# The first batch's W2 products in a four-stage residual kernel: rounded part first, remainder part later

## The reference, cut to what matters

```
x = x + quantise(x)                       # 8 groups: clip(round(x/d)+zp)..., chosen by |x| <= threshold
x = x + x @ W1[a(b)].T                    # W1: 8 matrices of 1024x1024, one chosen per batch
x = x + x @ W2.T + (x @ lora_A[l(b)]) @ lora_B.T * 0.5
x = x + (x @ B3[a(b)].T) @ A3[a(b)].T
```

## Time and profile before

| what | value |
|---|---|
| runs of the kernel before | median 486.1 us (485.64 to 488.54, 3 runs) |
| the profiled execution's own time | 486.4 us |
| its span | 484.6 us, 8214 instructions |
| busy: PE, DVE, ACT | 465.8 us (96%), 418.6 us (86%), 359.5 us (74%) |
| moved by the transfers | 67.07 MB |

### The profile page before, as it was taken

One profiled execution on the slowest core, in us unless ns is written; L12 is line 12 of the kernel. 1 busy time (PEld: TensorE's weight loads), 2 busy tenths in 40 slices (PEclk: granted clock), 3 DMA queues, 4 the chain that ended last, 5 costly groups with the idle time before them and its releaser, 6 DMA issues.

```text
span 484.6 us, 8214 instructions
## 1 busy us (share of the span) xinstructions
PE 465.8 (96%) x3184; PEld 426.1 (88%) x3184; DVE 418.6 (86%) x480; ACT 359.5 (74%) x384; POOL 45.2 (9%) x46
## 2 busy tenths in 40 slices
PE   3999769999999999999999999999999999999997
PEld 3969669899898989899998989899999989899995
DVE  3999999988999899989999899989999899989120
ACT  5989968679787879679787879679787879676011
POOL 1054001200003000200002000200002000100000
PEclk9999979999999999999999999999999999999999
DMA  7997314712236113712326113712336123702002
GB/s 276 402 415 243 131 34 148 292 45 103 90 95 284 43 60 131 276 60 103 106 91 268 44 62 127 287 49 103 118 93 254 43 73 116 289 5 87 1 1 87
DMA packets 17830, 67.07 MB, mean 138 GB/s; under 512 B 2576, under 2 KB 5904, under 8 KB 13712
## 3 DMA queue, kind: packets, MB, share of 16 engines
q1 hardware_dynamic: 17808, 66.81, 37.7%
HBM read 56.84 MB, written 9.96 MB: 138 GB/s over the span
## 4 chain that ended last, share of the span: by engine, by line
PE 83%; DVE 8%; ACT 4%; DMA 2%; issue 1%; POOL 0%; DVEq 0%; SPq 0%; ACTq 0%
PE x_bank L598 45%; PE acc L623 32%; DVE y L460 4%; PE x_bank L611 3%; PE acc L635 2%; PE acc L633 2%; DVE uq L448 1%; ACT tq L329 1%; DMA ua<-w2t 1%; DMA xin<-x 1%; DVE x L473 1%; DVE uq L466 1%; ACT mask L344 1%; DVE tq L439 1%; ACT w2h L400 1%
## 5 line engine op out<-in xcount | busy, mean ns | idle before, releaser
L598 PEld LDWEIGHTS x_bank<-x,w1b 128*128 128x128 f32 x2048 | 234.4, 194 | 8.1 <-issue 4.4
L598 PE MATMUL x_bank<-x,w1b 128*128 128x128 f32 x2048 | 235.8, 277 | 4.0 <-DVE x L473 4.0
L329 ACT ACTIVATE tq<-xin,magic,rdelta 128x1024 f32<-128x1024 f32 x128 | 157.0, 1234 | 3.7 <-DMA xin<-x 3.4
L344 ACT ACTIVATE mask<-absx,negtop 128x1024 bf16<-128x1024 f32 x112 | 128.5, 1147 | 40.8 <-DVE y L460 40.1
L460 DVE COPY_PREDICATED y<-mask,uq 128x1024 f32<-128x1024 int16 x112 | 150.7, 1346 | 0.1
L439 DVE TENSOR_SCALAR tq<-tq,par 128x1024 f32<-128x1024 f32 x128 | 98.5, 769 | 8.5 <-ACT tq L329 4.8
L448 DVE TENSOR_SCALAR uq<-tq,ylow,yhigh 128x1024 f32<-128x1024 f32 x112 | 92.5, 826 | 1.1 <-issue 0.9
L623 PE MATMUL acc<-w2h,x2h 128*128 128x512 f32 x256 | 80.9, 393 | 3.3 <-DVE x2l L479 3.3
L623 PE MATMUL acc<-w2h,x2l 128*128 128x512 f32 x256 | 79.9, 389 | 0.0
L623 PE MATMUL acc<-w2l,x2h 128*128 128x512 f32 x256 | 79.1, 390 | 0.0
L295 POOL TENSOR_TENSOR w1b<-w1b,eye 128x256 f32<-128x256 f32 x32 | 34.6, 1083 | 370.9 <-DMA w1b<-w 370.9
(11 more groups left out here) (56 smaller groups left out, 219.3 us busy)
## 6 DMA issues: line engine op xcount, KB each, us to landing
w1b<-w SPq DMA_DIRECT2D x32, 1024.0 KB, 6.7
xin<-x SPq DMA_DIRECT2D x16, 512.0 KB, 3.7
out<-outb SPq DMA_DIRECT2D x14, 512.0 KB, 2.8
w1b<-w2n SPq DMA_DIRECT2D x4, 1024.0 KB, 10.8
ring<-w2t SPq DMA_DIRECT2D x6, 512.0 KB, 6.3
ua<-e_dram SPq DMA_DIRECT2D x16, 128.0 KB, 2.5
ua<-w2t SPq DMA_DIRECT2D x2, 512.0 KB, 7.2
va<-la SPq DMA_DIRECT2D x8, 128.0 KB, 2.7
```

The source lines that it names most:

```text
L329: nc.scalar.activation(tq[:, n % TQ, :], flat(xin, c % UN), ACT.Identity, bias=magic[:, 0:1], scale=rdelta[:, g:g + 1]).then_inc(t_ready, 1)
L344: nc.scalar.activation(mask[:, n % MK, :], absx[:, :], ACT.Relu, bias=negtop[:, g:g + 1], scale=1.0).then_inc(mask_ready, 1)
L598: last = nc.tensor.matmul(x2_bank[2 * t + i][:, o % HALF * P:(o % HALF + 1) * P], w1b[:, o, at:at + P], x1[:, t, k, :], start=(o % HALF == ...
```

## The change

1. `stage` is rotated: `ua` is now the last stage. W2's blocks are loaded and rounded in the order 4, 5, 6, 7, 0, 1, 2, 3; then 4, 5, 6, 7 are loaded a second time. A stage is loaded again in the first round when its block is rounded (`w2h_ready`), in the second when the remainder of its block is made.
2. DVE makes no remainder in steps 10 to 13. It makes them in the order 3, 0, 1, 2, 4, 5, 6, 7 at steps 18, 19, 20, 21, 22, 26, 26, 27.
3. `ACT_V, DVE_V` go from 14, 15 to 17, 18, in every batch.
4. TensorE's first batch does HIGH alone, for both units (unit 0 in the order 0, 1, 2, 4, 5, 6, 7, 3). LOW follows behind unit 1: blocks 3, 0, 1, 2, 4 for both units at the end of the batch, blocks 5, 6, 7 for each unit in batch 1, behind six tiles of its first `w1_x1` and ahead of the `u_low` of that unit. Batch 1 is written out, the loop starts at 2. Batch 1 has six tiles ahead of the `u_low` where the others have three.
5. SP's first batch is written out in a new order; POOL adds four diagonals (the reloaded blocks) between the four of W1 of batch 1.

```diff
-        stage = [ua[:, :]] + [ring[:, i, :] for i in range(ST - 1)]
+        stage = [ring[:, i, :] for i in range(ST - 1)] + [ua[:, :]]
...
+        W2_BLOCK = (4, 5, 6, 7, 0, 1, 2, 3, 4, 5, 6, 7)
+        W2_PLACE = (0, 1, 2, 3, 0, 1, 2, 3, 0, 1, 2, 0)
+        W2_REST = (3, 0, 1, 2, 4, 5, 6, 7)
+        REST_SOON = 5
...
+            def load_w2(i):
+                if ST <= i < KT:
+                    sp.wait_ge(w2h_ready, i - ST + 1)
+                elif i >= KT:
+                    sp.wait_ge(w2l_ready, i - KT + 2)
+                sp.dma_start(stage[W2_PLACE[i]], w2t[W2_BLOCK[i], :, :]).then_inc(stage_in[W2_PLACE[i]], 16)
...
+            sp.wait_ge(x1_ready, 2)
+            load_x(1, 1)
             sp.wait_ge(e_out, 16 * EH)
-            sp.wait_ge(w2l_ready, ST + 1)
+            sp.wait_ge(w2l_ready, 1)
             load_u(a0)
+            a1, lab1 = ids_of(1)
+            for j in range(PAIRS):
+                sp.wait_ge(w1_used, j + 1)
+                load_w1(a1, j)
+                if j < PAIRS - 1:
+                    load_w2(KT + j)
+            sp.wait_ge(vl_ready, 2)
+            load_v(a1, lab1)
+            load_w2(KT + PAIRS - 1)
+            sp.wait_ge(ul_ready, 1)
+            load_u(a1)
+            sp.wait_ge(x1_ready, UN + 1)
+            load_x(2, 0)
...
+            for j in range(PAIRS):
+                w1_diagonal(1, j)
+                if j < PAIRS - 1:
+                    w2_diagonal(KT + j)
+            w2_diagonal(KT + PAIRS - 1)
+            with pool.Fori(2, B) as b:
...
-        ACT_W2, DVE_W2 = (9, 10, 11, 12, 13, 14, 15, 16), (10, 11, 12, 13, 18, 19, 20, 21)
+        ACT_W2, DVE_W2 = 9, (18, 19, 20, 21, 22, 26, 26, 27)
...
-        ACT_V, DVE_V = 14, 15
+        ACT_V, DVE_V = 17, 18
...
+                for at, k in zip(DVE_W2, W2_REST):
+                    if n == at:
+                        i = len(W2_BLOCK) - 1 - W2_BLOCK[::-1].index(k)
+                        dve.wait_ge(w2h_ready, W2_BLOCK.index(k) + 1)
+                        dve.wait_ge(w2_diag, i + 1)
+                        nc.vector.tensor_tensor(w2l[:, k, :], stage[W2_PLACE[i]], w2h[:, k, :].bitcast(f32),
+                                                ALU.subtract).then_inc(w2l_ready, 1)
...
+            def rest(t, order):
+                for i in order:
+                    pe.wait_ge(w2l_ready, i + 1)
+                    product(t, W2_REST[i], LOW)
+
+            def start_batch(b, u_at, second=False):
+                pe.wait_ge(x1_ready, UN * b + 1)
+                w1_x1(b, 0, range(u_at))
+                for t in range(UN):
+                    if second:
+                        rest(t, range(REST_SOON, KT))
+                    u_low(b - 1, 2 * t)
+                    u_low(b - 1, 2 * t + 1)
+                w1_x1(b, 0, range(u_at, OT))
...
+            def first_batch():
+                pe.wait_ge(x1_ready, 1)
+                w1_x1(0, 0, range(OT))
+                pe.wait_ge(g_ready, 2)
+                for k in (0, 1, 2, 4, 5, 6, 7, 3):
+                    if k in (0, HALF):
+                        pe.wait_ge(x2l_ready, k // HALF + 1)
+                    pe.wait_ge(w2h_ready, W2_BLOCK.index(k) + 1)
+                    product(0, k, HIGH)
+                pe.wait_ge(e_ready, 2 * EH)
+                second_unit(0, HIGH, first=True)
+                for k in range(HALF, KT):
+                    product(1, k, HIGH)
+                for t in range(UN):
+                    rest(t, range(REST_SOON))
...
+            first_batch()
+            start_batch(1, 6, second=True)
+            w2_x2(1)
+            second_unit(1)
+            for k in range(HALF, KT):
+                product(1, k)
+            with pe.Fori(2, LAST) as b:
                 batch(b)
-            batch(LAST, last=True)
+            last_batch()
```

More of the change, by code:

```diff
@@ L241, in _, with during @@
                 sp.dma_start(e_dram.rearrange("(h a) r n -> h (a r) n", h=EH)[h], outb[:, h, :]).then_inc(e_out, 16)
+            sp.wait_ge(x1_ready, 2)
+            load_x(1, 1)
             sp.wait_ge(e_out, 16 * EH)
-            sp.wait_ge(w2l_ready, ST + 1)
+            sp.wait_ge(w2l_ready, 1)
             load_u(a0)
-            def during(b, first, second):
+            a1, lab1 = ids_of(1)
[11 more added lines that the diff above has]
+            load_x(2, 0)
+            def during(b, second):
                 a, lab = ids_of(b + 1)
-                if not first:
-                    store(b - 1, 0)
-                    store(b - 1, 1)
+                store(b - 1, 0)
+                store(b - 1, 1)
                 sp.wait_ge(vl_ready, 2 * (b + 1))
@@ L264, in during @@
                     load_x(b + 2, 0)
-            during(0, True, True)
             with sp.Fori(1, LAST - 1) as b:
-                during(b, False, True)
-            during(LAST - 1, False, False)
+                during(b, True)
+            during(LAST - 1, False)
             store(LAST - 1, 0)
@@ L300, in _ @@
                 w2_diagonal(j)
-            for k in range(PAIRS, KT):
-                w2_diagonal(k)
-            with pool.Fori(1, B) as b:
+            for i in range(PAIRS, KT):
+                w2_diagonal(i)
+            for j in range(PAIRS):
[4 more added lines that the diff above has]
+            with pool.Fori(2, B) as b:
                 for j in range(PAIRS):
@@ L396, in tables @@
                                              ACT.Copy).then_inc(g_ready, 1)
[L397 to L400, removed]
+                if ACT_W2 <= n < ACT_W2 + KT:
+                    i = n - ACT_W2
+                    act.wait_ge(w2_diag, i + 1)
+                    nc.scalar.activation(w2h[:, W2_BLOCK[i], :], stage[W2_PLACE[i]], ACT.Copy).then_inc(w2h_ready, 1)
                 for e in range(2 * EH):
@@ L636, in u_low @@
                                  skip_group_check=True).then_inc(acc_done, 1)
-            U_AT = 3
-            def batch(b, first=False, last=False):
-                pe.wait_ge(x1_ready, UN * b + 1)
[L642 to L663, removed]
+            def rest(t, order):
+                for i in order:
+                    pe.wait_ge(w2l_ready, i + 1)
+                    product(t, W2_REST[i], LOW)
@@ new lines, in start_batch, with w2_x2 @@
+            def start_batch(b, u_at, second=False):
+                pe.wait_ge(x1_ready, UN * b + 1)
+                w1_x1(b, 0, range(u_at))
[5 more added lines that the diff above has]
+                w1_x1(b, 0, range(u_at, OT))
+            def w2_x2(b):
+                pe.wait_ge(x2l_ready, BANKS * b + 1)
+                pe.wait_ge(out_ready, ACCS * (b - 1) + 2)
+                for k in range(HALF):
+                    product(0, k)
+                pe.wait_ge(x2l_ready, BANKS * b + 2)
+                for k in range(HALF, KT):
+                    product(0, k)
@@ L664, in batch, with second_unit @@
+            def second_unit(b, parts=ALL, first=False, early=HALF):
                 pe.wait_ge(x1_ready, UN * b + 2)
                 w1_x1(b, 1, range(OT))
[L666 to L669, removed]
                 pe.wait_ge(vl_ready, 2 * (b + 1))
@@ L674, in batch, with last_batch @@
                     pe.wait_ge(out_ready, ACCS * b)
-                early = HALF // 2 if last else HALF
                 for k in range(early):
-                    product(1, k)
+                    product(1, k, parts)
                 pe.wait_ge(x2l_ready, BANKS * b + 4)
                 v_x2(range(HALF, KT))
[L680 to L688, removed]
-                    for k in range(early, KT):
-                        product(1, k)
+            def first_batch():
[13 more added lines that the diff above has]
+                    rest(t, range(REST_SOON))
+            def batch(b):
+                start_batch(b, 3)
+                w2_x2(b)
+                second_unit(b)
+                for k in range(HALF, KT):
+                    product(1, k)
+            def last_batch():
+                early = HALF // 2
+                start_batch(LAST, 3)
+                w2_x2(LAST)
+                second_unit(LAST, early=early)
+                for h in range(2):
+                    for k in range(early, KT):
+                        product(1, k, ALL, (h,))
+                    if h == 0:
+                        u_low(LAST, 0)
+                        u_low(LAST, 1)
+                    u_low(LAST, 2 + h)
             bilinear()
@@ L694, in _ @@
             adapters_e()
-            batch(0, first=True)
-            with pe.Fori(1, LAST) as b:
+            first_batch()
+            start_batch(1, 6, second=True)
+            w2_x2(1)
+            second_unit(1)
+            for k in range(HALF, KT):
+                product(1, k)
+            with pe.Fori(2, LAST) as b:
                 batch(b)
-            batch(LAST, last=True)
+            last_batch()
 def kernel(**inputs):
```

15 lines of the change are left out of this document (3 added, 12 removed).

## The result

The changed kernel takes 495.26 us (median of 4 runs, 494.39 to 495.6), the kernel before 486.07 (median of 4): the ratio is 1.018, 95% interval 1.014 to 1.021. It is slower by 9.2 us, where 489.6 was forecast with a range up to 492.8. The profiled span grew from 484.6 to 493.8 us, by the same 9.2.

The account below looks back on a forecast made before the run. The prediction took TensorE as full from about 73 us on. It summed 0.1 up to batch 1, 2.7 for deferred products and 0.7 for V to +3.5 us, giving 489.6 us, 0.7% slower, range 485.5 to 492.8.

Parts of the forecast that it names:

- What bounds the kernel now: TensorE is full from about 73 us on; only two earlier pauses and a clock loss, 9.7 us at most, can be won.
- Part 1: Ahead of x1 of unit 1: ScalarE's x2h limits, so 1.6 us won and x1 ends at 65.4 instead of 67.0.
- The stage buffer, loaded earlier now: ScalarE ahead of x1 of unit 1: 0.27 us of waiting for the stage buffer would be won.
- Part 2: TensorE until x1 of unit 1: waits about 4.9 us for x1 instead of 3.75, and the 2.7 us clock loss stays.
- Part 3: VectorE up to x1 of unit 2: ends at 99.0, was 97.7; TensorE starts batch 1 0.1 us later.
- Part 4: Batch 1: six deferred products cost TensorE 2.7 us; VectorE's three late remainders fit.
- Part 5: V moved in every batch: 0.13 us a batch, nearly 0.7 for six, ends 0 and 3.2; SP's later loads cost nothing.
- Rival C: V at step 18 costs its full 0.53 us in six batches, 3.2 instead of 0.7: 492.1 us; chance 0.13.
- Part 6: Four reloads adding 2 MB: block 4 is ready between 79 and 81 us, just in time, costed at nothing.
- A: VectorE, not ScalarE, limits ahead of x1 of unit 1; x1 comes 5 us earlier, about 486 us; chance 0.12.
- B: The reload of block 4 comes late, almost 5 us of waiting ahead of x1 of unit 2: 494 us; chance 0.1.
- D: POOL's diagonals hold VectorE out for their whole length, 4.5 instead of 1.2 us before x1 of unit 2: 492.9; chance 0.07.

Follow-up runs that it names:

- e5: e1 with ScalarE's four copies of the E tables moved from steps 12 to 14 to steps 16 and 17; 489.03 us.
- e2: The kernel before with only the V splits of batches 1 to 7 moved to steps 17 and 18; 489.59 us.
- e9: e1 plus four blocks' unit-0 remainder products ahead of the x2l wait, without the six deferred products in batch 1; 490.11 us.
- e3: The changed kernel with SP issuing load_x ahead of the load_v that waits for V, in every loop batch; 492.91 us.
- e1: The changed kernel with the V splits of batches 1 to 7 back at steps 14 and 15; 491.75 us.
- e12: The changed kernel itself, unedited, run again on another occasion; 495.32 us.

## Why the prediction was wrong, point by point

The sum gave 0.1 us up to batch 1, 2.7 in it and 0.7 for V in six batches, 3.5 in all. Measured are 1.9, 2.4 and 4.9, together 9.2. The largest miss is the last term.

- **What bounds the kernel now** held: TensorE is full behind 73 us, and what it is made to wait there is paid.
- **Part 1 (ScalarE limits x1 of unit 1)** was right in mechanism, and e5 showed it. Its size was off: x1 ended at 66.45 instead of 65.4, 0.6 earlier than before. That is the end that the prediction gave for "only the V copies", 66.5. The gain is no larger than the scatter: the changed kernel run again has 67.49, and e2, with the first batch of the kernel before, 65.99. The 0.85 us of ScalarE's waiting that the sum took as won did go, but ScalarE came as much later, as it waited for POOL behind transfers:

```profile
40.58 1.06 ACT L427 ACTIVATE w2h<-ua 128x1024 fp32r<-128x1024 f32 x1 [0.49 <-POOL ua L312]
...
43.15 1.14 ACT L371 ACTIVATE mask<-absx,negtop 128x1024 bf16<-128x1024 f32 x1
...
44.51 1.06 ACT L427 ACTIVATE w2h<-ring 128x1024 fp32r<-128x1024 f32 x1 [0.22 <-POOL ring L312]
...
55.79 0.59 ACT L380 ACTIVATE x2h<-x_bank 128x512 fp32r<-128x512 f32 x1
```

  The mask is back at 43.15 with no wait in front of it, where it was 43.10; ScalarE runs without a break to 55.79 but for 0.22. "The stage buffer, loaded earlier now" failed too: block 0 was issued at 35.14 and added to at 44.02, 8.9 us; before, the block in its place was issued at 37.24 and added to at 42.48. The transfers' share was 0.96 or more from 34 to 42 us, and the earlier issue gave no earlier landing.
- **Part 2** was right about the two pauses in kind (2.16 and 3.16 us, forecast 2.7 and 4.9; the HIGH products between them ran at half clock and so filled the rest) and about the half clock behind them.
- **Part 3** gave 33.56 us from x1 of unit 1 to x1 of unit 2, and 33.58 were measured (33.2 to 34.0 in the other profiles of this program). That it fits so well is partly luck. POOL's eight diagonals stretched VectorE by 1.9 us instead of the former three's 1.05, so by 0.8 and not 1.2 more, and 0.39 us of waiting for block 4's diagonal, put at nothing, made up for it. What it missed is TensorE's own arrival. "That the clock falls or not does not matter here" was said of the first pause; there was a second one, ahead of x2l of unit 1, with a second drop. +1.9 instead of +0.1, of which 1.05 comes from part 1 and 0.8 from this:

```profile
65.23 1.22 DVE L500 TENSOR_TENSOR x<-xin,uq 128x1024 f32<-128x1024 f32 x1
...
98.81 1.22 DVE L500 TENSOR_TENSOR x<-xin,uq 128x1024 f32<-128x1024 f32 x1
```

- **Part 4** gave 2.7, measured 2.4, but for half a reason: it said that VectorE's late remainders fit, and e9 shows that they would have cost a good part of it alone, 1.5 us in its profile.
- **Part 5 is the step that failed.** It gave 0.7 us with 3.2 as its end; the runs show 4.9 (profiles) and 2.9 to 4.1 (medians). Two terms of it failed. The larger is its "No cost" for SP, whose `load_v` now waits for step 18 ahead of `load_x`: it looked at when x is wanted, not at what x's transfer does to the next one. e3 puts 3.0 of the 4.9 there. The smaller is the slack. V's 0.53 was right, but the 0.40 us between the end of x1 and TensorE's start was not all slack. Where TensorE waits for x1 it still starts 0.14 us behind its end (e3: 158.26 to 158.40), and its first 48 matmuls then take 5.62 us instead of 5.52. The six pairs of the kernel before stand 0.38 to 0.56 apart, so about 0.3 us of slack on the mean. That leaves about 0.3 us a batch for V where the sum had 0.13: 1.9 us in e3 instead of 0.7. Rival C, V's full 0.53 in six batches, was too small for the first reason.
- **Part 6** nearly held: block 4, costed at nothing, was 0.39 us late in the trace.

```profile
81.70 1.23 DVE L540 TENSOR_TENSOR w2l<-ring,w2h 128x1024 fp32r<-128x1024 f32 x1 [0.39 <-POOL ring L312]
```

- **Rivals.** A did not come (e5: ScalarE was the limit). B did not come. D did not: eight diagonals of 8.4 us in all stretched VectorE by 1.9, the largest stretch beside one diagonal in that part was 0.5 us, and POOL's own ops took 0.64 to 1.57. The prediction read the lock rule of the Trainium skill, "SBUF — State Buffer", section "Who interferes with whom", as the whole length of every diagonal put on VectorE. That section says that the op that issues first keeps the shared ports and the other one blocks until it ends, so it charges whichever starts second, and only for the rest of the first. The trace agrees on who pays: the `tq` at 141.88 started 0.39 us behind POOL's op and was stretched; the one below started 0.07 us ahead of it and kept its 0.74 us, and POOL's op took 1.26 instead of 0.73. On the size it differs a little: at 141.88 POOL's op had 0.66 us left, and the stretch was 0.46.

```profile
378.82 0.74 DVE L466 TENSOR_SCALAR tq<-tq,par 128x1024 f32<-128x1024 f32 x1
```

```profile
378.89 1.26 POOL L317 TENSOR_TENSOR w1b<-w1b,eye 128x256 f32<-128x256 f32 x1 [1.68 <-DMA w1b<-w]
```

## What to carry to other kernels

When a step is moved in a program that repeats, price everything that queues behind its signal on the issuing engine, and follow each transfer to the compute op that its landing will meet: here a transfer's landing moved by two us, with ample slack to its user, cost more than the instruction that was moved. Work deferred out of a stage that waits into one that is full is paid there: 2.4 us here, and leaving the products out gave back only about half of it, as the next engine was nearly full too. Relieving one engine ahead of a join is worth only what the next engine at that join leaves; VectorE shed 5 us, and x1 came 0.6 earlier. And a distance between a signal and the start that waits for it is not all slack: compare it with the distance where the engine really waits.

## What the runs showed of the hardware that was not expected

- The length of a pause does not tell whether TensorE's clock falls behind it. One of 3.27 us ahead of 57.68 left it at full rate, while pauses of 2.16 and 2.69 us in the changed kernel had matmuls at half rate behind them (1.05 us a pair instead of 0.62). Two executions with the same instructions up to there and the same pause of 3.02 us ahead of unit 1 differ as well: in e1 the 128 matmuls behind it took 14.53 us, in e12 16.16.
- What a POOL diagonal (0.73 us alone) costs a VectorE op depends on which of them starts first and on the op. Where POOL was ahead, a `tensor_scalar` lost what POOL's op had left, less 0.2 to 0.3 us (0.66 left and 0.46 lost at 141.88, 0.57 left and 0.31 lost for the clamp at 156.21), the fused op of L493 lost 0.33 and the selection 0.25 (1.34 to 1.59 at 251.02). Where VectorE was 0.1 us or more ahead, `tq`, the clamp and the selection lost nothing and POOL's op grew, to 1.85 us beside the selection at 305.95. The `x2l` that reads PSUM took its 0.69 us in either order.
- W1's pair of 1 MB landed 4.7 to 4.9 us after its issue with x 3.9 us ahead of it in the queue (the kernel before, six rounds), and 5.5 to 7.0 us with x 2.2 us ahead (the changed kernel, six rounds).
